# Rows for the expert gathers turned back by TensorE and copied by ScalarE, and two scan products moved from GpSimd to VectorE

## The reference, cut to what matters

```
S = S * exp(g_t); delta = (v_t - k_t @ S) * b_t          # gated delta rule, step by step
S = S + outer(k_t, delta); o_t = q_t @ S
...
x = x + ga * attention(h)
h = layernorm(x) * (1 + cb) + sb                          # cb, sb: one row per sequence
logits = h @ Wr + br; probs = softmax(logits)
top_vals, top_idx = top_k(probs, 3)                       # 12 experts, 3 for each token
x = x + gb * experts(h, top_idx, ...)                     # 256 -> 640 -> 256, relu
```

## Time and profile before

| | |
|---|---|
| median of 3 runs | 816.49 us |
| the profiled execution | 817.62 us |
| its span | 815.5 us |
| TensorE busy | 754.3 us (92%) |
| VectorE busy | 543.1 us (67%) |
| ScalarE busy | 266.4 us (33%) |
| GpSimd busy | 230.0 us (28%) |
| first gathered rows turned by TensorE (line 1688) | at 629.95 us |

### The profile page before, as it was taken

One profiled execution on the slowest core, in us unless ns is written; L12 is line 12 of the kernel. 1 busy time (PEld: TensorE's weight loads), 2 busy tenths in 40 slices (PEclk: granted clock), 3 DMA queues, 4 the chain that ended last, 5 costly groups with the idle time before them and its releaser, 6 DMA issues. The chain is left out here.

```text
span 815.5 us, 11539 instructions
## 1 busy us (share of the span) xinstructions
PE 754.3 (92%) x4011; PEld 554.7 (68%) x4011; DVE 543.1 (67%) x1321; ACT 266.4 (33%) x420; POOL 230.0 (28%) x194
## 2 busy tenths in 40 slices
PE   5989999999999999999999498998977999999995
PEld 4422323477888888887456387877843999999995
DVE  4798995467555555555799999999687453343445
ACT  2466678453343434343571111121231000000000
POOL 4442000022232323231030000867042344344421
PEclk9999999999999999999999799999999999999997
DMA  8595000101111111140122405200014999999972
GB/s 298 150 216 102 3 2 2 59 21 39 39 48 48 52 45 54 43 156 1 33 84 78 193 1 162 72 1 1 1 52 163 358 346 326 344 344 350 349 246 77
DMA packets 39333, 101.04 MB, mean 124 GB/s; under 512 B 5374, under 2 KB 19894, under 8 KB 38326
## 3 DMA queue, kind: packets, MB, share of 16 engines
q1 hardware_dynamic: 35334, 91.06, 34.2%
q0 software_dynamic: 3504, 8.98, 3.0%
q10 hardware_dynamic: 448, 0.39, 0.2%
HBM read 84.17 MB, written 16.44 MB: 123 GB/s over the span
## 5 line engine op out<-in xcount | busy, mean ns | idle before, releaser
L1383 PE MATMUL psum<-xr,wr 128*128 128x512 f32 x600 | 145.5, 393 | 1.0 <-DVE arena L2039 1.0
L1383 PEld LDWEIGHTS psum<-xr,wr 128*128 128x128 f32 x600 | 113.6, 190 | 25.3 <-issue 1.7
L735 POOL TENSOR_TENSOR wr<-ring,wr 128x512 fp32r<-128x512 f32 (+1 forms) x50 | 54.9, 1117 | 235.3 <-ACT wr L924 145.9
L1699 PEld LDWEIGHTS psum<-arena 128*128 128x128 f32 x700 | 83.5, 192 | 3.3 <-issue 1.5
L1699 PE MATMUL psum<-arena 128*128 128x128 f32 x700 | 83.9, 275 | 1.1 <-ACT arena L1136 1.1
L1709 PE MATMUL psum<-arena 128*128 128x256 f32 x350 | 81.3, 379 | 0.0
L2504 DVE TENSOR_SCALAR arena<-psum,arena 128x256 f32<-128x256 f32 x35 | 16.9, 484 | 93.0 <-PE psum L1709 93.0
L1394 PE MATMUL psum<-hr,wr 128*128 128x512 f32 x300 | 76.6, 391 | 0.9 <-DVE hr L1976 0.9
L1887 DVE TENSOR_REDUCE small<-psum 128x1 f32<-128x512 f32 x112 | 71.0, 685 | 6.8 <-PE psum L1259 6.2
L2002 DVE TENSOR_TENSOR hid<-hid,psum 128x512 f32<-128x512 f32 x50 | 34.4, 687 | 58.6 <-ACT hid L930 58.4
L899 ACT ACTIVATE arena<-psum 128x1024 f32<-128x1024 f32 x64 | 63.0, 1023 | 26.9 <-PE psum L1269 26.1
(11 more groups left out here) (391 smaller groups left out, 1235.9 us busy)
## 6 DMA issues: line engine op xcount, KB each, us to landing
arena<-in_w1u SPq DMA_DIRECT2D x35, 642.5 KB, 5.9
arena<-in_w1d SPq DMA_DIRECT2D x35, 640.0 KB, 5.5
ring<-in_w SPq DMA_DIRECT2D x25, 384.0 KB, 3.0
z_scratch<-w_a SPq DMA_DIRECT2D x4, 768.0 KB, 7.2
arena<-z_scratch SPq DMA_DIRECT2D x8, 384.0 KB, 7.2
arena<-part_scratch SPq DMA_DIRECT2D x9, 256.0 KB, 7.2
qkv_scratch<-arena SPq DMA_DIRECT2D x4, 512.0 KB, 2.7
arena<-qkv_scratch SPq DMA_DIRECT2D x4, 512.0 KB, 4.0
```

The source lines that it names most:

```text
L735: pool.tensor_tensor(wr0[:, k, LO, part], ring0[:, k, part], wr0[:, k, HI, part], ALU.subtract).then_inc(s["w0_lo"], 1)
L1383: ins = pe.matmul(bank[2 * b + m][:, :], wr0[:, k, w, lo:lo + P], xr[:, x, f, half(b)], start=(f == 0 and (w, x) == PARTS[0]), stop=(f == ...
L1699: ins = pe.matmul(bank[2 + r % 2 * 3 + k // 2][:, tile(k % 2)], wup1[:, r % NW, lo:lo + P], xgT[:, r % 2, f, :], start=(f == 0), stop=(f = ...
```

## The change

GpSimd forms only v = 0 and 1 of the first unit of 4, and then waits for VectorE's first reduction before it starts on `w_og`. VectorE forms v = 2 and 3 of that unit ahead of the four of the second, and waits for the sums of the sixth unit (whose buffer is used again) first. Both reductions now need VectorE's own products.

GpSimd's four instructions on `xn` (790, 791) are gone. In their place TensorE turns `hT` back with 16 transposes, right after the second logits, into banks 0 to 3, four to a bank, and ScalarE copies each bank to `xn` with one instruction, after the two Exps of the softmax and ahead of the third Exp. The 16 dummy matmuls that stood there are 8. SyncE's four stores wait for a copy each. One semaphore has a new name.

```
@@ SyncE
             for i in range(0, NT, 2):
-                sp.wait_ge(s["ones"], 4 + B + i // TB + 1)
+                sp.wait_ge(s["act_rows"], 2 + i // 2)
@@ GpSimd
-                for v in range(VV):
+                for v in range(VV if u < SUMMED else VV // 2):
                     ins = state_product(pool, u, v) if u < SUMMED else last_product(pool, 0, v)
                 ins.then_inc(s["state_prod"], 1)
+            pool.wait_ge(s["scan_lo"], 2 * (NB - 1) + 1)
...
-            for b in range(B):
-                x = xn[:, b * TB:(b + 1) * TB, :].rearrange("p t (f d) -> p t f d", f=KD)
-                pool.wait_ge(s["ln_tr"], B * 3 + b + 1)
-                ch.link(pool.tensor_tensor(x, x, row_of(2, b).unsqueeze(1).broadcast_to((P, TB, KD, P)), ALU.mult))
-                pool.tensor_tensor(x, x, row_of(1, b).unsqueeze(1).broadcast_to((P, TB, KD, P)), ALU.add)\
-                    .then_inc(s["ones"], 1)
@@ ScalarE
+            for m in range(NT // 2):
+                act.wait_ge(s["y_tr"], NT // 2 * 3 + m + 1)
+                act.activation(xn[:, 2 * m:2 * m + 2, :], bank[m].rearrange("p (t d) -> p t d", t=2), ACT.Copy)\
+                   .then_inc(s["act_rows"], 1)
@@ TensorE
             logits(1)
-            warm(16, 7)
+            for m in range(NT // 2):
+                for x in range(2):
+                    for f in range(KD):
+                        ins = pe.transpose(bank[m][:, x * D + f * P:x * D + (f + 1) * P],
+                                           hT[:, f, tile(2 * m + x)], ident[:, :])
+                ins.then_inc(s["y_tr"], 1)
+            warm(8, 7)
@@ VectorE
-            dve.wait_ge(s["state_sum"], 1)
+            dve.wait_ge(s["state_sum"], SUMMED - 1)
+            for v in range(VV // 2, VV):
+                last_product(dve, 0, v)
             for v in range(VV):
                 ins = last_product(dve, 1, v)
             formed = ch.mark(ins)
             dve.wait_ge(s["state_prod"], SUMMED + 1)
             for n in range(2):
                 n0, count = UNITS[SUMMED + n]
-                if n:
-                    ch.need(formed)
+                ch.need(formed)
```

More of the change, by code:

```diff
@@ L990, in _ @@
                 ins = act.activation(taps[:, n, :], ident[:, :], ACT.Identity, scale=cols[:, w:w + 1])
-            ins.then_inc(s["taps"], 1)
+            ins.then_inc(s["act_rows"], 1)
             def conv_silu(n):
@@ L1492, in _ @@
                     ins.then_inc(s["proj"], 1)
-            pe.wait_ge(s["taps"], 1)
+            pe.wait_ge(s["act_rows"], 1)
             def conv_v(n):
```

## The result

Over 20 runs of each kernel in turn, the changed one takes 813.48 us (median, 810.74 to 817.44) and the kernel before 819.04 us (815.89 to 826.44). The ratio is 0.9929, with a 95% interval of 0.9908 to 0.9950: about 5.8 us, or 4.1 to 7.5. Forecast were 6.95 us, a ratio of 0.9915, and 809.5 us as the time. The gain lies in the interval; the time came out 4.0 us above the forecast and just above the range (813.2). The kernel before had moved too: 819.04 us in these runs against 816.49 in the three that the forecast started from.

What follows compares the result with a forecast made beforehand. The expert tiles on TensorE were taken as the largest stage, so whatever ends earlier ahead of them counts whole. 1.9 + 3.2 + 0.4 + 1.45 = 6.95 us, from 816.49 to 809.5 us; range 807.8 to 813.2.

Steps and rivals of the forecast that it cites:

- The waits behind GpSimd: Norm and softmax, 595 to 607 us: VectorE's long instructions wait until GpSimd's instruction ends, since both share a port.
- The sum's base: The median of the kernel before, 816.49 us, from which the whole gain of 6.95 us was subtracted to give 809.5 us.
- The idle 2.2 us of part 2: TensorE's turning of the second sequence can begin at 597.57 instead of 599.77 us, without the idle time: 2.2 us.
- part 2: Norm of the second sequence without GpSimd's instructions beside it: the turning ends at 598.55 instead of 601.74 us, 3.2 us earlier.
- The clock term of part 2: The 8 transposes turning the second sequence take 1.0 instead of 1.97 us at full clock: 1.0 us, bounds 0 and 1.0.
- Part 3: Softmax: ScalarE's table load ends last before Exp, so 0.4 of 1.05 us comes through; line 2411 shortens by 1.45 us.
- Part 1: Last products ahead of `gather(3)`: VectorE forms six at 0.40 us each, 2.4 us; gain 1.9 us, 0.7 us slack left.
- The new wait and w_og: GpSimd's wait for the first reduction delays `w_og` to 569.4 from 567.40 us; its readers have more than 2 us in hand.
- Part 4: Added transposes, dummies, copies and stores cost nothing; TensorE keeps 2.0 us idle, four copies take 0.60 us each.
- What doesn't move along: Gathers and weight loads shift with VectorE's tables; nothing from there to the expert tiles hangs on anything older.
- The clock rival: TensorE falls to half clock at the tables' matmuls or first expert tiles, costing about 1.7 us: 810.5 to 812.2 us; 13%.
- The largest stage: The expert tiles, lines 1699, 1709 and 1688, with 18% of the span, entered by the chain at about 630 us.

Runs made afterwards that it cites:

- the controls: The changed kernel run again, unaltered, in two later comparisons with the kernel before; ratios 0.9898 and 0.9912.
- w_og at once: The changed kernel without GpSimd's wait for the first reduction ahead of `w_og`; ratio 0.9940 to the kernel before, first last product to `gather(3)` 7.49 us.

## Why the prediction was right in its mechanism and wrong in its time

- **The waits behind GpSimd** (parts 2 and 3): right. All four went with GpSimd's instructions and came back with them on other data.
- **The sum's base**: wrong, and this is what put the time out of the range. The step was "the median to 816.49 - 6.95 = 809.5 us". The range was drawn round three runs that lay within 0.6 us; 20 runs of the same kernel spread over 10.5 us with a median of 819.04. 819.04 - 6.95 = 812.1 would have left 1.4 us of error, and with the old base even the gain as measured, 5.8 us, would have given 810.7 us, well inside the range. The prediction's "a measurement tells about 0.2%" was too narrow for the same reason: with 20 runs each the ratio is known to 0.2% either way, and with 3 the base was 2.5 us off. At least part of the spread is TensorE's clock upstream, at 66 to 74 and 170 to 180 us; why it falls is open.
- **The idle 2.2 us of part 2**: right, in every profile without GpSimd's work.
- **The clock term of part 2**, 1.0 us: mis-sized. It was in the profile that I worked from (3.2 us up to the end of the turning, as forecast), but in the four other executions with GpSimd's work in that place, one of them with filling, "norm" is 41.05 to 41.21 us. Against those the rows gain 4.3 us and not the 5.1 forecast. Where there was no filling the clock fell too, but after most of the turning was done, where it cost 0.2 us at most up to the ranks. That the fall hit the turning in the first profile was chance.
- **Part 3**: right to 0.05 us. The load ended last, Exp followed it at once, and 1.45 us came from line 2411.
- **Part 1**, 1.9 us: 1.45 to 1.50 measured. The product's own cost was taken as 0.40 us from its end behind GpSimd's; alone it lasts 0.61 to 0.62 us and the next starts 0.53 us after it. So about 0.2 us of a product's own time pass while it waits. That made the six 3.27 and not 2.4 us, and the limit of 0.52 us named in the prediction was passed. The slack of 0.7 us became a wait of 0.45.
- **The new wait and w_og**: right that it is hidden, and underrated: without it part 1 would have been worth nothing.
- **Part 4, the added work**: right. 2.20 us of idle time were left where 2.0 had been forecast, and the copies took 0.5 us each.
- **What doesn't move along**: incomplete. "Nothing between there and the tiles hangs on anything older" is true, but the clock at the tables and the first gather's place behind the weights make this stretch 17.8 to 20.3 us long. The clock rival foresaw its place and price of up to 1.7 us; the second profile of the kernel before has the same trouble, so it blurs the times more than it takes from the gain.
- **The largest stage**: misread, without consequence for the sum. The expert tiles have the largest share of the chain, but the chain in time order begins only at 562.79 us. Lines 1383 and 1394 keep TensorE busy from 172 to 382 us, longer than the tiles' 631 to 796 us.

With the two mis-sized terms put right, 4.3 + 1.5 = 5.8 us is what the ratio of 0.9929 gives. That they agree so closely is partly luck: the interval allows 4.1 to 7.5 us, and the controls gave 8.4 and 7.2 us.

## What to carry to other kernels

Lay the timelines of VectorE and GpSimd side by side and look for one instruction with two durations; what is short elsewhere is a wait, and it counts whole wherever it is on the path. If such a neighbour is moved or made to wait, ask what follows it on its engine: here `w_og` would have taken its place. Work out the gain in stretches between fixed instructions, take them from more than one execution where the clock has a part in them, and don't set a range for the absolute time by three runs that happen to agree: forecast the difference, and give the base a range of its own.

## What the runs showed of the hardware that was not expected

- A VectorE product of 128x256 that waits for GpSimd ends 0.40 us after it, but has 0.61 us alone: 0.2 us of it pass during the wait.
- GpSimd's two instructions for `w_og` took 3.01 us beside VectorE's products before, 2.74 us in w_og at once, and 2.49 us in the changed kernel, beside no more than a reduction of VectorE. So GpSimd seems to wait for VectorE too; no experiment was made for it alone.

```profile
571.99 2.49 POOL L783 TENSOR_TENSOR w_og<-arena,rows_mod 128x512 f32<-128x512 f32 x2 [4.99 <-DVE hid L2346]
```

- After the same idle time of 2.20 us ahead of the same 8 transposes they took 1.97 us in one execution and 1.25 in another of the same kernel: the clock fell to 0.50 in both, 0.7 us before they began in the one and 0.8 us after in the other.
- The same instructions at 66 to 74 us took 2.7 and 3.3 us longer in two profiles where the granted clock there was 0.79 than in the first profile of before, where it was 1.00.
